# Layer 1's probabilities transposed by a DMA, and another plan of its stage times

## The reference, cut to what matters

```
xn  = layernorm(x) * (scale1 + 1) + shift1
q, k, v = split(xn @ Wqkv.T + bias)              # 16 heads of 32
qn, kn = q / |q| * sm, k / |k|
p   = softmax(qn @ kn.T + mask)                  # per sequence and head, 64 x 64
x   = x + ((p @ v) @ Wproj.T + bproj) * gamma1
h   = gelu((layernorm(x) * (scale2 + 1) + shift2) @ Wfc1.T + bfc1)
x   = x + (h @ Wfc2.T + bfc2) * gamma2
```

## Time and profile before

| what | value |
|---|---|
| median of three runs | 2703.53 us (2703.23 to 2704.87) |
| the profiled execution's own time | 2702.99 us |
| its span, first to last instruction | 2701.0 us |
| layer 0, up to about | 1390 us |
| layer 1's first attention block | 1433 to about 1566 us |
| one block of layer 1 after it, as the pitch of its scores | 147.5 us, seven times |
| mean granted TensorE clock | 0.974 of full speed |

### The profile page before, as it was taken

One profiled execution on the slowest core, in us unless ns is written; L12 is line 12 of the kernel. 1 busy time (PEld: TensorE's weight loads), 2 busy tenths in 40 slices (PEclk: granted clock), 3 DMA queues, 4 the chain that ended last, 5 costly groups with the idle time before them and its releaser, 6 DMA issues.

```text
span 2701.0 us, 47110 instructions
## 1 busy us (share of the span) xinstructions
PE 2539.2 (94%) x18448; PEld 1268.9 (47%) x18448; DVE 1378.7 (51%) x2138; ACT 947.1 (35%) x1546; POOL 1041.3 (39%) x1007
## 2 busy tenths in 40 slices
PE   6699999999999999999996689999999999999998
PEld 5344444444544444454443345454545445454543
DVE  5455253442524435243245657575857576675741
ACT  3343132231313223132132354453626263534542
POOL 1223232222313223132113456564656556555632
PEclk8899999999999999999997799999999999999999
DMA  5520101001010010100222101212120212121110
GB/s 191 166 81 5 49 3 40 15 5 49 3 51 3 15 38 3 50 3 18 65 103 96 44 21 47 65 29 84 29 76 25 73 40 56 41 58 55 34 54 28
DMA packets 112788, 129.00 MB, mean 48 GB/s; under 512 B 51662, under 2 KB 53966, under 8 KB 112596
## 3 DMA queue, kind: packets, MB, share of 16 engines
q1 hardware_dynamic: 112596, 126.07, 15.6%
HBM read 71.63 MB, written 18.74 MB: 33 GB/s over the span
## 4 chain that ended last, share of the span: by engine, by line
PE 73%; issue 10%; DVE 7%; POOL 5%; ACT 4%; DMA 0%; POOLq 0%; SPq 0%; DVEq 0%; ACTq 0%
PE ps_m L1525 37%; PE ps_abef L1525 18%; PE ps_d L1525 3%; PE ps_c L1525 2%; PE ps_abef L1713 2%; PE ps_abef L1715 2%; PE ps_abef L1720 2%; PE ps_abef L1747 1%; PE ps_d L1701 1%; POOL h_mlp L875 1%; POOL inner L897 1%; DVE weights L1211 1%; PE ps_c L1566 1%; ACT weights L987 1%; POOL scratch L928 1%
## 5 line engine op out<-in xcount | busy, mean ns | idle before, releaser
L1525 PE MATMUL ps_m<-h_mlp,weights 128*128 128x512 f16 x3072 | 707.3, 382 | 40.1 <-POOL h_mlp L875 19.1
L1525 PE MATMUL ps_m<-weights,inner 128*128 128x512 f16 x3072 | 690.4, 379 | 8.7 <-DVE scratch L1365 8.7
L1525 PEld LDWEIGHTS ps_m<-h_mlp,weights 128*128 128x128 f16 x3072 | 296.3, 98 | 385.7 <-issue 37.7
L1525 PEld LDWEIGHTS ps_m<-weights,inner 128*128 128x128 f16 x3072 | 296.8, 98 | 346.2 <-DVE scratch L1365 6.5
L897 POOL TENSOR_TENSOR inner<-scratch,inner 128x512 f16<-128x512 f32 x256 | 301.1, 1176 | 320.7 <-ACT inner L1064 320.7
L1525 PE MATMUL ps_abef<-h_mlp,weights 128*128 128x512 f16 x1536 | 345.4, 379 | 0.4 <-DVE scratch L1365 0.4
L1525 PEld LDWEIGHTS ps_abef<-h_mlp,weights 128*128 128x128 f16 x1536 | 147.6, 98 | 173.8 <-DVE scratch L1365 1.3
L1064 ACT CAST inner<-scratch 128x512 f16<-128x512 f32 x256 | 156.6, 612 | 106.2 <-DVE scratch L1493 68.1
L866 POOL TENSOR_TENSOR scratch<-scratch 128x1 f32<-128x1 f32 x128 | 30.1, 235 | 360.2 <-ACT scratch L1006 304.7
L875 POOL TENSOR_TENSOR h_mlp<-scratch,h_mlp 128x512 f16<-128x512 f32 x64 | 74.0, 1156 | 207.1 <-ACT h_mlp L1021 207.1
L1363 DVE SCALAR_TENSOR_TENSOR scratch<-scratch,ps_m 128x512 f32<-128x512 f32 x64 | 44.0, 687 | 187.7 <-ACT scratch L1076 187.7
(11 more groups left out here) (167 smaller groups left out, 3676.3 us busy)
## 6 DMA issues: line engine op xcount, KB each, us to landing
x_mlp<-x_attn SPq DMA_DIRECT2D x64, 256.0 KB, 2.3
weights<-gamma SPq DMA_DIRECT2D x128, 128.0 KB, 3.0
scratch<-scratch SPq DMA_DIRECT2D x128, 128.0 KB, 2.7
x_attn<-x SPq DMA_DIRECT2D x32, 256.0 KB, 2.7
x_mid<-x_mlp SPq DMA_DIRECT2D x32, 256.0 KB, 2.1
x_attn<-x_mid SPq DMA_DIRECT2D x32, 256.0 KB, 2.8
out<-x_mlp SPq DMA_DIRECT2D x32, 256.0 KB, 2.2
inner<-wada_t SPq DMA_DIRECT2D x4, 1024.0 KB, 6.4
```

The source lines that it names most:

```text
L1525: ins = nc.tensor.matmul(o, left(a, k), right(b, k), start=(first and n == 0), stop=(last and n == len(order) - 1), skip_group_check=True)
```

## The change

For each of the 32 tiles of layer 1, `turn_p` on PE and both halves of `key_major` go, and SP issues one DMA that transposes all of `p1` (128 x 2048 float16, 512 KB) from SBUF to SBUF into `pt1`. It waits for `p_lo` of the tile and for `mix` of the tile before; `mix` waits for it, and so does the next `p_hi`, which overwrites `p1`. The order of nearly all stages of layer 1 is another, as the planned times are. The stage `turn` no longer waits for the copies but for `mask` of the tile before, and two waits are added that guard the inverse norms. Waits and stages not shown are as before.

```diff
-NORM_AT = [0.0, 1.7, 3.0, 5.3, 6.9, 5.7, 5.4, 7.5]
+NORM_AT = [0.0, -0.1, 2.5, 4.1, 7.0, 7.4, 7.9, 10.1]
 CHAIN = [(s + "1", at) for s, at in zip(NORM, NORM_AT)] + [
-    ("proj", 10.1), ("square", 11.9), ("projv", 14.3), ("v_hi", 16.4), ("sums", 17.5), ("v_lo", 20.1), ("inv_q", 21.1),
-    ("inv_k", 21.8), ("unit_q", 23.5), ("turn", 26.6), ("unit_k", 26.8), ("t_hi", 28.7), ("t_lo", 30.9),
-    ("spread", 32.9), ("gamma_a", 32.9), ("scores", 33.1), ("exp", 33.3), ("mask", 34.3), ("soft", 36.9),
-    ("p_hi", 37.6), ("p_lo", 42.5), ("key_major", 47.0), ("turn_p", 47.6), ("c_hi", 49.0), ("mix", 50.2),
-    ("c_lo", 52.1), ("out", 52.4), ("add", 56.8), ("gate", 56.9)]
-PE_COST = {... "turn_p": 0.9,
+    ("proj", 10.8), ("square", 13.1), ("projv", 13.7), ("v_hi", 17.7), ("sums", 19.2), ("v_lo", 19.5), ("inv_q", 20.0),
+    ("inv_k", 24.0), ("unit_q", 24.5), ("unit_k", 26.3), ("t_hi", 26.4), ("turn", 26.5), ("t_lo", 28.7),
+    ("scores", 29.9), ("gamma_a", 32.7), ("mask", 35.2), ("exp", 35.7), ("p_hi", 37.7), ("spread", 37.9),
+    ("soft", 39.0), ("turn_p", 39.3), ("p_lo", 40.3), ("c_hi", 48.9), ("mix", 49.2), ("c_lo", 51.4), ("out", 51.8),
+    ("add", 53.6), ("gate", 56.0)]
...
-("u", -0.1), ("tanh", 2.4), ("arg", 3.2), ("m_hi", 4.0), ("gelu", 5.7), ("m_lo", 6.4)
+("u", -0.3), ("tanh", 2.2), ("arg", 2.9), ("m_hi", 4.5), ("gelu", 4.8), ("m_lo", 6.5)
-("d", 4.3), ("y", 4.8), ("store", 5.0)
+("d", 1.8), ("y", 2.3), ("store", 2.4)
...
-FIRST1 = ... attention_plan([0.0, 26.4, 53.1, 79.8], [59.0, 108.1, 123.5, 165.6])
-STEADY1 = with_mlp(attention_plan([0.0, 26.2, 52.7, 79.2], [108.0, 96.5, 122.9, 136.6]))
+FIRST1 = ... attention_plan([0.0, 24.6, 52.1, 77.3], [63.1, 96.1, 115.7, 151.1])
+STEADY1 = with_mlp(attention_plan([0.0, 24.9, 53.3, 78.3], [112.8, 96.2, 116.7, 134.8]))
...
 SP
+                if stage == "turn_p":
+                    turned, mixed = counts(tile(it, t) + 1, tile(it, t))
+                    sp.wait_ge(s_l1k, 1)
+                    sp.wait_ge(L1.p_lo, turned)
+                    sp.wait_ge(L1.mixed, mixed)
+                    sp.dma_start(pt1, p1.rearrange("p g h t -> p (g h t)"), transpose=True).then_inc(L1.pt, 16)
 POOL, inv_k
+                    pool.wait_ge(L1.nmax, n + 1)
 ACT
-                    act.wait_ge(L1.p_turned, n)
+                    act.wait_ge(L1.pt, 16 * n)
                     nc.scalar.copy(p1[:, :, 0, :], e1).then_inc(L1.p_hi, 1)
-                if stage == "key_major":
-                    act.wait_ge(L1.p_turned, n + 1)
-                    act.wait_ge(L1.mixed, n)
-                    nc.scalar.copy(pt1[:, 0:HALF, :], as16(ps_m[2], HALF)).then_inc(L1.pt, 1)
 DVE
+                    dve.wait_ge(L1.npow, n)
...
-                if stage == "key_major":
-                    dve.wait_ge(L1.p_turned, n + 1)
-                    dve.wait_ge(L1.mixed, n)
-                    nc.vector.tensor_copy(pt1[:, HALF:, :], as16(ps_m[3], HALF)).then_inc(L1.pt2, 1)
 PE
                     pe.wait_ge(L1.normed, 2 * n + 2)
-                    pe.wait_ge(L1.pt, n)
-                    pe.wait_ge(L1.pt2, n)
+                    pe.wait_ge(L1.masked, n)
...
-                if stage == "turn_p":
-                    pe.wait_ge(L1.p_lo, n + 1)
-                    for g in range(HEADS1):
-                        ins = nc.tensor.transpose(as16(ps_m[2 + g // HALF], HALF)[:, g % HALF, :],
-                                                  p1[:, g].rearrange("p h t -> p (h t)"), ident16[:])
-                    ins.then_inc(L1.p_turned, 1)
                 if stage == "mix":
-                    pe.wait_ge(L1.pt, n + 1)
-                    pe.wait_ge(L1.pt2, n + 1)
+                    pe.wait_ge(L1.pt, 16 * (n + 1))
```

More of the change, by code:

```diff
@@ L167 @@
 NORM = ["stat", "rstd", "scale", "turn_x", "gain", "shift", "hi", "lo"]
-NORM_AT = [0.0, 1.7, 3.0, 5.3, 6.9, 5.7, 5.4, 7.5]
+NORM_AT = [0.0, -0.1, 2.5, 4.1, 7.0, 7.4, 7.9, 10.1]
 CHAIN = [(s + "1", at) for s, at in zip(NORM, NORM_AT)] + [
-    ("proj", 10.1), ("square", 11.9), ("projv", 14.3), ("v_hi", 16.4), ("sums", 17.5), ("v_lo", 20.1), ("inv_q", 21.1),
-    ("inv_k", 21.8), ("unit_q", 23.5), ("turn", 26.6), ("unit_k", 26.8), ("t_hi", 28.7), ("t_lo", 30.9),
-    ("spread", 32.9), ("gamma_a", 32.9), ("scores", 33.1), ("exp", 33.3), ("mask", 34.3), ("soft", 36.9),
-    ("p_hi", 37.6), ("p_lo", 42.5), ("key_major", 47.0), ("turn_p", 47.6), ("c_hi", 49.0), ("mix", 50.2),
-    ("c_lo", 52.1), ("out", 52.4), ("add", 56.8), ("gate", 56.9)]
-PE_COST = {"turn_x1": 0.45, "turn_x2": 0.45, "proj": 5.4, "projv": 2.8, "turn": 0.9, "scores": 1.4, "turn_p": 0.9,
+    ("proj", 10.8), ("square", 13.1), ("projv", 13.7), ("v_hi", 17.7), ("sums", 19.2), ("v_lo", 19.5), ("inv_q", 20.0),
[3 more added lines that the diff above has]
+    ("add", 53.6), ("gate", 56.0)]
+PE_COST = {"turn_x1": 0.45, "turn_x2": 0.45, "proj": 5.4, "projv": 2.8, "turn": 0.9, "scores": 1.4,
            "mix": 0.9, "out": 2.8}
@@ L206, in emit @@
         if kind == "up" and k == KC - 1:
-            merged.extend((now + at, s, j) for s, at in (("u", -0.1), ("tanh", 2.4), ("arg", 3.2), ("m_hi", 4.0),
-                                                         ("gelu", 5.7), ("m_lo", 6.4)))
+            merged.extend((now + at, s, j) for s, at in (("u", -0.3), ("tanh", 2.2), ("arg", 2.9), ("m_hi", 4.5),
+                                                         ("gelu", 4.8), ("m_lo", 6.5)))
         if kind == "down" and k == IC - 1:
-            merged.extend((now + at, s, j) for s, at in (("d", 4.3), ("y", 4.8), ("store", 5.0)))
+            merged.extend((now + at, s, j) for s, at in (("d", 1.8), ("y", 2.3), ("store", 2.4)))
     for at, s, t in plan:
@@ L224, in with_mlp @@
     return [m[1:] for m in sorted(merged, key=lambda m: (m[0], order[id(m)]))]
-FIRST1 = [m[1:] for m in attention_plan([0.0, 26.4, 53.1, 79.8], [59.0, 108.1, 123.5, 165.6])]
-STEADY1 = with_mlp(attention_plan([0.0, 26.2, 52.7, 79.2], [108.0, 96.5, 122.9, 136.6]))
+FIRST1 = [m[1:] for m in attention_plan([0.0, 24.6, 52.1, 77.3], [63.1, 96.1, 115.7, 151.1])]
+STEADY1 = with_mlp(attention_plan([0.0, 24.9, 53.3, 78.3], [112.8, 96.2, 116.7, 134.8]))
 MLP1 = ("up", "down", "gamma_m", "u", "arg", "tanh", "gelu", "m_hi", "m_lo", "d", "y", "store")
@@ L241 @@
         "bank d": [("turn_x1", "gain1"), ("turn_x2", "gain2"), ("out", "gate")],
-        "banks e and f": [("turn", "t_lo"), ("scores", "mask"), ("turn_p", "key_major")],
+        "banks e and f": [("turn", "t_lo"), ("scores", "mask")],
         "moments": [("stat1", "scale1"), ("stat2", "scale2")],
@@ L246 @@
         "norm_sq": [("sums", "inv_k")], "norm_inv": [("inv_q", "unit_k")], "qk1": [("square", "turn")],
-        "qkt": [("t_hi", "scores")], "e1": [("mask", "p_lo")], "p1": [("p_hi", "turn_p")], "pt1": [("key_major", "mix")],
+        "qkt": [("t_hi", "scores")], "e1": [("mask", "p_lo")], "p1": [("p_hi", "turn_p")], "pt1": [("turn_p", "mix")],
         "ctx1": [("c_hi", "out")], "v1": [("v_hi", "spread")], "vv1": [("spread", "mix")], "gated": [("gate", "add")],
@@ L528, in __init__ @@
                     self.t_lo = s("qk_feature_major_lo")
-                    self.pt2 = s("p_key_major_second_half")
         L0, L1 = Layer(0), Layer(1)
```

## The result

The changed kernel takes 2710.16 us, median of 7 runs (2708.21 to 2713.30). The kernel before took 2703.23 us in 7 runs beside them (2696.51 to 2707.62). The ratio is 1.0028, with a 95% interval of 1.0017 to 1.0039: slower by 0.28%. The forecast was 2696.0 us, faster by 0.3%: it had the wrong sign, though the time lies in its wide range of 2675 to 2780. The profiled execution took 2708.75 us, 2707.0 of it span (before: 2701.0).

The account below looks back on a forecast made before the run. PE was taken to set layer 1's pace. Terms -25.2 (transposes), +14.7 (`turn1` waits), +6 (`mix1` waits) and -3 (first block) gave -7.5 us: 2696.0 us by the median, range 2675 to 2780.

Parts of the forecast that it names:

- The step that failed: On SP, `gamma_m` and `store1` behind the new DMA wait a few us, with over 8 in hand; priced at nothing.
- The 25.2 us off PE: Layer 1's 28 tiles under an MLP each lose a 0.90 us slot of transposes on PE: -25.2 us.
- D = 4.6 us: Time from the end of `p_lo` to `mix` with the transposing DMA; taken as 4.6 us, bounds 3.2 and 23.
- the walk through tile 0: New list timed from `scores0`: `mask0` starts 3.8, `p_hi0` ends 12.9, `p_lo0` 15.3, `unit_k1` 23.0; PE at `turn1` 20.9.
- The waits at `turn1`, 14.7 us,: PE reaches `turn1` before its input and waits 2.1 us a block, +14.7 us over seven blocks.
- The waits at `mix1`, 6 us,: PE waits 0.8 us at `mix1` for the DMA in each of seven blocks, +6 us.
- the prediction's signs of being wrong: Wrong if D, from `p_lo` end to `mix`, exceeds 5, or `scores2` or `proj1`, taken as on time, waits every block.
- The first block: Layer 1's first block, where PE idles for want of input, gains: -3 us, between -8 and +3.
- Much slower: Rival: D, from `p_lo` end to `mix`, of 10 to 23 us; 2990 at 15, about 3250 at 23; chance 0.15.
- upper bound of 23: Time from `p_lo` end to `mix` if `pt1` is written in 16,384 pieces of 32 bytes: 23 us.
- Slower, PE waits at `mix`: Rival: DMA delay D beyond what the order leaves; 2711 at 6, 2765 at 8; chance 0.25 for 6 to 9.
- no change: Rival: D, from `p_lo` end to `mix`, of 5 to 6 us uses up the gain: 2698 to 2709 us; chance 0.15.

Follow-up runs that it names:

- The first experiment: Changed kernel with the planned offset of `store` put back from 2.4 to 5.0, so SP issues `gamma_m` ahead of it: 2691.45 us, ratio 0.9944.
- the second: Kernel before, transposes still on TensorE, with the offset of `store` 0.0 in place of 5.0, ahead of the next `gamma_m`: 2743.67 us, ratio 1.0150.
- The fourth experiment: Kernel before, its old stage order kept, with the transposes and copies replaced by the transposing DMA on SP: 2739.76 us, ratio 1.0137.
- the third experiment: Changed kernel's new stage order, with the transposes on TensorE and the two copies in place of the DMA: 2740.15 us, ratio 1.0140.

## Why the prediction was wrong

**The step that failed** is the one on SP: "Behind it `gamma_m` and `store1` wait a few us, with over 8 us in hand by the planned times. Both at nothing". I looked at what stands behind the new DMA, and not at what the planned times had done to the order of the old ones: `store` is now ahead of `gamma_m`, and with it a hand-over that waits twice for landings. It was priced at nothing. By the planned times `gamma_m` of tile 3 had 12.65 us to `d` of its tile (132.75 to 145.4); in the trace the chain ahead of it took 6.7 us (1852.19 to 1858.86) and was begun late, and its own landing another 4.7 (to 1863.53). Measured, PE's wait for `d` grew by 17.0 - 5.5 = 11.5 us, and the clock at half behind three of these holes cost 1.3 to 1.6 us in a block. The first experiment takes both away and gets 14.7 us of span back; the second puts the same order into the kernel before and loses 39.5. The first one's ratio of 0.9944 on the 2703.53 us of before gives 2688, the lower end of the forecast's own range of 2688 to 2700. That it is the lower end has its cause below, in two waits that were priced too high.

**The clock** is a term that the sum did not have at all. I took an idle microsecond as a microsecond. In the six blocks it is 4.8 us in all.

**The 25.2 us off PE** were there: PE's busy time in a block fell from 146.28 to 142.80, 3.5 against 3.6, where the clock is full.

**D = 4.6 us** was right, in part by luck. In the block at 2044.9, `p_lo0` ends at 2059.78 and `mix0` starts at 2064.35: 4.57 us. But 4.6 had been worked out for the landing alone, from copies that do not transpose. The DMA lands 4.3 us after its issue, and the hand-overs before and behind it, some 0.3, were left out. The timeline of that block holds the walk through tile 0:

```profile
2044.94 0.97 PE L1746 MATMUL ps_abef<-scratch 32*64 32x64 f16 x96
...
2064.35 0.73 PE L1759 MATMUL ps_c<-weights,scratch 128*32 128x64 f16 x64
...
2067.57 1.09 PE L1735 MATMUL ps_abef<-ident,weights 128*128 128x128 f32 x8 [1.09 <-DVE weights L1397]
...
2048.77 1.22 DVE L1454 TENSOR_TENSOR weights<-ps_abef,scratch 128x1024 f32<-128x1024 f32 x1
...
2056.53 1.04 ACT L1132 CAST scratch<-weights 128x1024 f16<-128x1024 f32 x1 [1.90 <-DVE weights L1466]
...
2057.65 2.13 POOL L952 TENSOR_TENSOR scratch<-weights,scratch 128x1024 f16<-128x1024 f32 x1 [2.31 <-ACT scratch L1132]
...
2059.84 1.79 SPq L808 DMA_TRANSPOSE weights<-scratch  x1
```

Counted from `scores0`: `mask0` at 3.8 (forecast 3.8), `p_hi0` done at 12.6 (12.9), `p_lo0` at 14.8 (15.3), `turn1` at 22.6 (23.0). So the walk through three engines' lists was good to half a microsecond.

**The waits at `turn1`, 14.7 us,** came out at 7.6: 1.1 in place of 2.1 a block. `turn1` started 0.4 us before the forecast time, and PE came to it 21.5 us after `scores0` in place of 20.9. Each of the two makes the wait shorter. PE's delay is small gaps ahead of it: at a matmul each 0.215 us, `proj1` would start at 2049.71 and starts at 2050.04 (in the block at 1744.7 a wait of 0.34 for the mask stands there, L1679), and `mix0` would start at 2064.07 and starts at 2064.35, when the DMA has landed. **The waits at `mix1`, 6 us,** came out at 1.5 for the DMA and 1.0 for `v_lo`. Here PE came 18.7 us after `scores1` in place of 17.9, and it had waited 0.4 on the way, at `proj` of tile 2 for `h_attn`, in every block. Such a wait in every block, at a stage that I took as on time, was one of the prediction's signs of being wrong. With `h_attn` and L1679 all these make 13.3 us against 20.7 forecast, so that the sum without the failed step was too careful by some 7 us in the blocks: 145.8 us apart in the first experiment, where 146.8 was forecast.

**The first block** came out as forecast. `scores` of the second block starts at 1598.4, before it was 1601.6, which is 3.2 less; 0.4 of that stands ahead of layer 1, so the block itself gave 2.8 where 3 were forecast. How the terms of that -3 came out one by one is not worked out; PE waits 13.5 us for the DMA there. From `scores` of the second block to the last block's `down` products (L1679, at 2657.66 and before at 2654.03) the kernel lost 6.8 us, and from there to the end 2.4: ahead of these products PE idles 4.14 us in place of 3.13, and the clock is at half in the 6.8 us from 2655.5, where before it is full. That is the 6.0 us between the spans. The loss in the last block was not in the sum either. The first experiment still has the 4.14 us and a clock of 0.53 in the 3.4 us behind them.

**The rivals.** "Much slower" is excluded: D is 4.6 us. (Its upper bound of 23 isn't the sum of its own terms, 3.2 and 22; nothing hangs on it.) The Trainium skill's figure of 1309 ns per 128x128 transpose by DMA (VectorE: DVE Perf Modes, The three transpose paths) put the time about 3200 where it was taken 16 times. One DMA of 16 blocks isn't 16 times that: 4.3 us for all, 0.27 us for each. The page's order of the two paths agrees with the trace: TensorE takes 0.90 us for the 16. The DMA pays here only because TensorE is the bound and the new order leaves it its 4.6 us. "Slower, PE waits at `mix`" (2711 at D = 6) and "no change" (2698 to 2709) name about the time that was measured, but not the mechanism: both need D over 5, and the kernel is slower with 1.5 us of such waits. The fourth experiment shows that mechanism in the old order.

**What stays open.** Why PE's clock fell after idle stretches of 4.69, 2.67 and 2.43 us at block starts, and did not after others of 2.63 and 2.92, no run here tells apart; nor why it fell after 4.14 us in the last block and not after 3.13 in the kernel before. Why `turn`, `mix` and `proj` wait twice as long with the transposes on TensorE in the third experiment is not taken apart either.

## What to carry to other kernels

When an order is planned anew, compare the old and the new list of every queue, the DMA queue's too, and for each pair that has changed places ask who waits for the one that is now behind; a store with a hand-over that waits for its landing must not stand ahead of a load that the bound engine's next bank hangs on. Two halves of a change that lose some 35 us each won 13 together here, so a transfer with latency and the order that makes room for it are tried as one. An engine that is idle a third of the time has still an order in which other engines' needs cross: the mask moved 2 us earlier, past one other stage, made what hangs on it 1.8 us later, and two instructions that now ran side by side on VectorE and GpSimd each took about a microsecond longer.

## What the hardware showed that was not expected

- A DMA that transposes 512 KB of two-byte values from SBUF to SBUF lands in 4.3 us, min 4.3 and max 4.5 over 32, and holds SP's queue for 1.63 to 2.07 us, where plain issues of 256 KB hold it for 0.34 to 0.53. The packets of the whole kernel rise from 112788 to 179343, 2,080 for each transpose: near the 2,048 runs of 256 bytes, and far from 16,384 pieces of 32.
- Two DMAs of half the size do not land sooner than the whole, 4.7 to 4.8 against 4.6 us from the end of `p_lo`: each lands 3.2 us after its issue, but the two issues together take SP 2.62 us.
- After PE's idle stretch of 6.01 us its granted clock was 0.50 for 6.8 us, in the kernel with the store first. PE was busy 5.92 of these, so this wait cost an estimated 3 us more in the clock behind it, half as much again.
- VectorE's `arg` (128x512 float32, SBUF to SBUF) takes 0.69 us, and 1.64 where GpSimd's L881 runs beside it; L881 then takes 2.14 in place of 1.17.
